# Attention inside a macaron block: the longest row's probabilities turned in squares of 32 by VectorE and moved on chip by 16 DMAs, a group's values weighed at once, the end batches' projections moved

## The chip, the cores and the metric

The kernel runs on one core of one Trainium2 chip. The metric is device time in microseconds (us); the kernel before has a median of 2754.09 us over 3 runs (2752.3 to 2754.87).

## The reference

The input x is 8 batches x 512 tokens x 512 features, all float32. Three stages follow each other:

```
x = x + 0.5 * ffn(layernorm(x))        # gate and up 512 -> 2048, silu, keep 2 of 4, down 2048 -> 512
x = x + attention(layernorm(x))
x = x + 0.5 * ffn(layernorm(x))        # the same weights again

attention: q = x @ w_q.T   (16 heads of 32)        k, v = split(x @ w_kv.T)   (one head, shared)
           q, k scaled and rotated;  a = q k^T, masked causally;  p = softmax(a)
           out = (p @ v) @ w_proj.T + b_proj
```

Only the attention in the middle is touched by this change.

## The kernel before

The engines run programs of their own, in a fixed order, and meet at semaphores. `ffn_phase` makes the first and the third stage; `attention_phase` makes the second.

**Groups, rows and units.** Attention goes through 8 batches. A batch has four groups of 4 heads, and a group has four rows: 128 queries each, of all 4 heads. By causality row i has i + 1 blocks of 128 keys. One (group, row) is a unit K; there are 16 in a batch and 128 in all. `ORDER = (0, 1, 2, 3)`: the shortest row comes first, the longest (row 3, 4 blocks, 512 keys) last.

**A unit's way.** `scores(K)` (PE, L1093): 4 matmuls, one for each head, into banks 0 to 3. `mask_scores` (DVE, L1353): adds the mask and takes the minimum, out to `probs`, one instruction for each head. `exps` (ACT, L1234): the exponential in place, with the sum. `turn_probs(K, j)` (PE, L1102): 4 transposes of 128x128 for block j, into one of three turning banks. `copy_turned`: that bank to `pt`, by ACT (L1239) or by DVE (L1359; `ON_VECTOR` says which blocks). `weigh(K)` (PE, L1117): the values times the turned blocks, 4 matmuls a block, two records each in the trace, into bank 6. After a group's last `weigh`, `scale_output` (DVE, L1372) divides by the sums, which `invert_sums` (DVE, L1365), `widen` (POOL) and `turn_sums` (PE, L1078) have made ready.

**The order of the work.** Every engine has a `step(K)`, written out by hand. PE's is: blocks 0 and 1 of unit K turned; the projection that `PROJECT` gives for this unit of the batch (keys and values of the next batch at unit 0, its queries at 1, 2, 5, 6, the output of the batch before at 9, 10, 13, 14); blocks 2 and up turned; the sums turned in the last unit of a group; at even units `weigh(K - 2)` and `weigh(K - 1)`; and `scores(K + 3)`. DVE's is: two heads of `mask_scores(K + 2)`, its copies, the other two heads, what a projection left in its bank (two instructions for queries, L1342 and L1345; one for an output, L1377), the sums' reciprocal, the scaling, and statistics for a later batch. `scores(K)` waits until all four heads of unit K - 1 are masked, since the banks are the same. `probs` has three buffers, `pt` holds rows 2 and 3 apart from rows 0 and 1.

**Queues.** All DMAs are issued by SP, in program order. In attention these are, for each batch, four stores of the finished x (L902), each after DVE's addition, and one load of a later x (1 MB, L894).

Of the kernel before, what the change touches and what calls it, by code (L numbers as in the profile page):

```python
# [26 lines left out]
P = 128  # L27
# [4 lines left out]
def macaron_kernel(nc, x_in, w_gu, w_d, w_q, w_kv, w_p, b_p, rotary_q, rotary_k, out):  # L32
# [35 lines left out]
    halves = place("halves", [P, TT], F32)  # L68
    stats = place("stats", [P, NB, TT, 6], F32)
# [3 lines left out]
    nmax = place("nmax", [P, 3, TT], F32)  # L73
# [56 lines left out]
    pt = place("pt", [P, 2 * TT, HG, P], F32)  # L130
# [21 lines left out]
    probs = place("probs", [P, 3, HG, S], F32)  # L152
# [7 lines left out]
    with ExitStack() as ctx:  # L160
# [60 lines left out]
        p_turned = sem("p_turned")  # L221
        pt_scalar = sem("pt_scalar")
# [567 lines left out]
        def attention_phase(src, dst, m0):  # L790
# [15 lines left out]
            ORDER = (0, 1, 2, 3)  # L806
            PLACES = ((7,), (5, 6), (0, 1, 2), (3, 4, 5, 6))
            ON_VECTOR = ((), (1,), (1,), (1, 3))
            TURN_X, TURN_KV, TURN_K = {11: 0, 12: 1, 13: 2, 14: 3}, 1, 4
            PROJECT = {0: ("kv", 0), 1: ("q", 0), 2: ("q", 1), 5: ("q", 2), 6: ("q", 3),  # L810
                       9: ("out", 0), 10: ("out", 1), 13: ("out", 2), 14: ("out", 3)}
# [3 lines left out]
            FINISH = {2: 0, 3: 1, 6: 2, 7: 3}  # L815
# [13 lines left out]
            def heads_of(ap):  # L829
                return ap.rearrange("p (h d) -> p h d", d=HD)  # L830

            def blocks_before(K, of):

                one = [sum(1 for j in range(i + 1) if of(i, j)) for i in ORDER]
                return K // TT * sum(one) + sum(one[:K % TT])
# [30 lines left out]
            for K in range(ALL):  # L866
                B, k = divmod(K, UNITS)
                nxt = B + 1
                next_turn("p", K, 0)
                if row_of(K) >= 1:  # L870
                    next_turn("p", K, 1)
                if k in PROJECT:
                    what, t = PROJECT[k]
                    if what == "out":
                        if B > 0:
                            next_turn("out", B - 1, t)
                    elif nxt < BATCHES:
                        next_turn(*(("kv", nxt) if what == "kv" else ("q", nxt, t)))
                for j in range(2, row_of(K) + 1):
                    next_turn("p", K, j)  # L880
# [10 lines left out]
            def sync(sp):  # L891
# [30 lines left out]
                sp.wait_ge(q_finished, BATCHES * NHG)  # L922
                load_raw(0)
                sp.wait_ge(k_step, BATCHES * KSTEP)
                sp.wait_ge(x_biased, BATCHES * TT)
                load_raw(1)
                store(BATCHES - 2)
# [8 lines left out]
            def gpsimd(g):  # L936
# [40 lines left out]
                def step(K):  # L977
# [6 lines left out]
                    if nxt < BATCHES:  # L984
                        if k in FINISH:
                            finish_q(nxt, FINISH[k])
# [33 lines left out]
            def tensor(pe):  # L1020
# [76 lines left out]
                def turn_probs(K, j):  # L1097
# [3 lines left out]
                    for s in range(HG):  # L1101
                        last = pe.transpose(ps[:, s * P:(s + 1) * P], probs[:, K % 3, s, j * P:(j + 1) * P], ident[:, :])  # L1102
                    last.then_inc(p_turned, 1)

                def weigh(K):

                    B, k = divmod(K, UNITS)
                    i = row_of(K)
                    pe.wait_ge(pt_scalar, blocks_before(K + 1, by_scalar))
                    pe.wait_ge(pt_vector, blocks_before(K + 1, by_vector))  # L1110
                    if k % TT == 0 and K >= TT:
                        pe.wait_ge(att_done, K // TT)
                    if k == 0:
                        pe.wait_ge(kvtok_done, B + 1)
                    for j in range(i + 1):
                        for s in range(HG):
                            last = pe.matmul(outs[s * HD:(s + 1) * HD, i * P:(i + 1) * P], kvtok[:, B % 2, j, 1],  # L1117
                                             pt[:, PLACES[i][j], s], start=(j == 0), stop=(j == i))
                    if k % TT == TT - 1:
                        last.then_inc(pv_done, 1)  # L1120
# [13 lines left out]
                def project(B, k):  # L1134

                    if k not in PROJECT:
                        return
                    what, t = PROJECT[k]
                    if what == "out":
                        if B > 0:  # L1140
                            project_out(B - 1, t, take_turn(("out", B - 1, t), x_summed, (B - 1) * TT + t + 1))
                    elif B + 1 < BATCHES:
                        if what == "kv":
                            project_kv(B + 1)
                        else:
                            project_q(B + 1, t)

                def step(K):
                    B, k = divmod(K, UNITS)
                    i, nxt = row_of(K), B + 1  # L1150
                    turn_probs(K, 0)
                    if i >= 1:
                        turn_probs(K, 1)
                    project(B, k)
                    for j in range(2, i + 1):
# [41 lines left out]
                weigh(ALL - 2)  # L1197
# [361 lines left out]
```

## Time and profile before

| | us |
|---|---|
| median of 3 runs | 2754.09 |
| the profiled execution | 2751.58 |
| its span | 2749.7 |
| PE busy | 2710.5 |
| DVE busy | 1852.4 |
| ACT busy | 1122.3 |
| POOL busy | 306.0 |
| granted TensorE clock, mean share | 0.997 |

The profiled execution lies 2.5 us under the median, and its span 1.9 us under its own time. In the span the first stage runs to about 1,090 us, attention to about 1,680 us, and the third stage to the end. A matmul's busy time is longer than the time until the next one starts, since they are pipelined, so a PE that is 99% busy can still have room; what a matmul costs is read from start to start.

The rows below come from the page, from the instructions in order of time (start, length, engine, line, operation, out<-in, and in brackets the idle time before it and what ended it), from tables by stretch (start:end, length, then for PE, PE's weight loads, DVE, ACT and POOL the busy time and the instructions, the granted clock as a share, the DMA engines' share, GB/s), and from the chain that ended last.

### The profile page before, as it was taken

The numbers are of one execution on the slowest core, as the hardware profiler recorded it, in microseconds if no ns is written. First come the engines' busy times: TensorE is split into PE (matmuls) and PEld (weight loads), VectorE is DVE, ScalarE is ACT, GpSimd is POOL, SyncE is SP. The second block draws the span as 40 slices with busy tenths as digits, with TensorE's granted clock in tenths as the row PEclk, the third lists the DMA queues.
The fourth block names the chain that finished last, engine by engine and source line by source line (L and its number), as shares of the span: only waits on it lengthen the run. The fifth ranks groups of instructions, "written<-read, shape, count | busy, mean of one in ns | idle before, by whom it ended". The sixth has DMA issues, their size and how long they took to land.

```text
span 2749.7 us, 41657 instructions
## 1 busy us (share of the span) xinstructions
PE 2710.5 (99%) x15520; PEld 2191.6 (80%) x15520; DVE 1852.4 (67%) x3538; ACT 1122.3 (41%) x2399; POOL 306.0 (11%) x318
## 2 busy tenths in 40 slices
PE   8999999999999999999999999999999999999999
PEld 6888888888888887677777768888888888888887
DVE  6667666765676667777777775667666766676655
ACT  4233333333333233777777784333333332333232
POOL 0000000000000004544444430000000000000000
PEclk9999999999999999999999999999999999999999
DMA  4210311121112111000000012211221132103100
GB/s 147 83 46 16 138 46 46 62 93 46 46 62 92 46 46 60 18 13 28 32 32 28 29 47 93 81 49 46 81 77 58 38 103 82 46 16 107 46 15 31
DMA packets 65069, 156.49 MB, mean 57 GB/s; under 512 B 6784, under 2 KB 7040, under 8 KB 64640
## 3 DMA queue, kind: packets, MB, share of 16 engines
q1 hardware_dynamic: 64896, 154.17, 16.7%
q8 instruction: 111, 1.82, 0.3%
q14 instruction: 62, 0.51, 0.1%
HBM read 128.97 MB, written 25.17 MB: 56 GB/s over the span
## 4 chain that ended last, share of the span: by engine, by line
PE 94%; DVE 3%; ACT 1%; POOL 1%; issue 0%; DMA 0%; SPq 0%; ACTq 0%; DVEq 0%; POOLq 0%
PE bank L391 50%; PE bank L412 25%; PE bank L1102 5%; PE bank L1070 3%; PE bank L1093 3%; PE bank L1117 3%; PE bank L1130 3%; PE bank L274 1%; DVE probs L1353 1%; PE bank L1045 1%; PE bank L1078 1%; POOL xnt_l L974 0%; PE bank L428 0%; DVE att L1372 0%; ACT hs_h L521 0%
## 5 line engine op out<-in xcount | busy, mean ns | idle before, releaser
L391 PE MATMUL bank<-xnt_h,wgu_h 128*128 128x512 f32 x2048 | 802.1, 392 | 4.2 <-ACT sg L507 2.8
L391 PE MATMUL bank<-xnt_h,wgu_l 128*128 128x512 f32 x2048 | 798.0, 390 | 0.0
L391 PE MATMUL bank<-xnt_l,wgu_h 128*128 128x512 f32 x2048 | 797.7, 389 | 0.0
L576 DVE TENSOR_TENSOR h<-bank,sg 128x512 f32<-128x512 f32 x256 | 176.8, 691 | 590.1 <-PE bank L391 574.4
L511 ACT ACTIVATE mag<-h 128x512 f32<-128x512 f32 x256 | 162.0, 633 | 715.6 <-DVE h L576 715.6
L391 PEld LDWEIGHTS bank<-xnt_h,wgu_h 128*128 128x128 f32 x2048 | 385.0, 188 | 84.4 <-ACT sg L507 3.7
L391 PEld LDWEIGHTS bank<-xnt_h,wgu_l 128*128 128x128 f32 x2048 | 384.9, 188 | 80.7
L391 PEld LDWEIGHTS bank<-xnt_l,wgu_h 128*128 128x128 f32 x2048 | 385.1, 188 | 78.3
L412 PE MATMUL bank<-wd_h,hs_h 128*128 128x512 f32 x1008 | 392.2, 389 | 0.0
L412 PE MATMUL bank<-wd_h,hs_l 128*128 128x512 f32 x1008 | 392.1, 389 | 0.0
L412 PE MATMUL bank<-wd_l,hs_h 128*128 128x512 f32 x1008 | 392.1, 389 | 0.0
L521 ACT CAST hs_h<-h 128x512 fp32r<-128x512 f32 x256 | 155.6, 622 | 510.8 <-DVE h L605 503.3
L1234 ACT ACTIVATE probs<-probs,nmax 128x384 f32<-128x384 f32 (+3 forms) x512 | 284.8, 560 | 2.0 <-DVE nmax L1353 1.8
L1353 DVE CUSTOM_DVE_ANT_0 probs<-bank,causal 128x384 f32<-128x384 f32 (+3 forms) x512 | 226.4, 485 | 43.3 <-PE bank L1093 43.0
L507 ACT ACTIVATE sg<-bank 128x512 f32<-128x512 f32 x256 | 153.0, 598 | 207.1 <-PE bank L391 206.6
L412 PEld LDWEIGHTS bank<-wd_h,hs_l 128*128 128x128 f32 x1008 | 189.2, 188 | 39.4
L412 PEld LDWEIGHTS bank<-wd_h,hs_h 128*128 128x128 f32 x1008 | 189.2, 188 | 39.3
L412 PEld LDWEIGHTS bank<-wd_l,hs_h 128*128 128x128 f32 x1008 | 189.2, 188 | 39.0
L281 POOL TENSOR_SCALAR var_eps<-meanvar 128x4 f32<-128x4 f32 x23 | 7.9, 342 | 1786.6 <-DVE meanvar L250 1786.6
L1102 PEld LDWEIGHTS bank<-ident,probs 128*128 128x128 f32 x1280 | 140.2, 142 | 73.7 <-ACT probs L1234 45.3
L1102 PE MATMUL bank<-ident,probs 128*128 128x128 f32 x1280 | 179.8, 282 | 7.0 <-ACT xt_raw L1226 5.2
L563 DVE SCALAR_TENSOR_TENSOR x_sb<-bank,x_sb 128x512 f32<-128x512 f32 (+1 forms) x256 | 159.1, 682 | 11.1 <-PE bank L412 5.8
(132 smaller groups left out, 3221.3 us busy)
## 6 DMA issues: line engine op xcount, KB each, us to landing
raw_gu<-in_w_gu SPq DMA_DIRECT2D x128, 512.0 KB, 4.9
raw_d<-in_w_d SPq DMA_DIRECT2D x128, 256.0 KB, 2.6
x_mid<-x_sb SPq DMA_DIRECT2D x64, 256.0 KB, 2.0
x_sb<-x_mid SPq DMA_DIRECT2D x10, 1024.0 KB, 5.5
x_sb<-in_x SPq DMA_DIRECT2D x32, 256.0 KB, 4.7
out<-x_sb SPq DMA_DIRECT2D x32, 256.0 KB, 2.1
x_sb<-x_mid SPq DMA_DIRECT2D x24, 256.0 KB, 4.9
raw_q<-in_w_q SPq DMA_DIRECT2D x1, 1024.0 KB, 5.0
```

Source lines behind the costliest of these rows:

```text
L391: last = pe.matmul(ps, w[:, r, kind, k], xs[:, b, k], start=(i == 0), stop=(i == 3 * KD - 1))
L412: last = pe.matmul(bank[DOWN + t][:, :], hs[:, b, r, tok], w[:, r], start=(i == 0), stop=(i == 3 * NR - 1))
L507: a.activation(sg[:, r % 2], bank[GATE + r % 2][:, :], ACT.Silu).then_inc(silu_done, 1)
L511: a.activation(mag[:, r], h[:, r], ACT.Abs).then_inc(mag_done, 1)
L521: a.copy(hs_h[:, b, r], h[:, r]).then_inc(hs_h_done, 1)
L563: v.scalar_tensor_tensor(out=x, in0=bank[banks + t][:, :], scalar=0.5, in1=x, op0=ALU.mult, op1=ALU.add).then_inc(added, 1)
L576: v.tensor_tensor(h[:, r], bank[UP + r % 2][:, :], sg[:, r % 2], ALU.mult).then_inc(h_done, 1)
L1070: last = pe.matmul(ps[:, :], w[:, k, cols], x[:, 0, k], start=(k == n == 0), stop=(k == KD - 1 and n == 2))
L1093: last = pe.matmul(bank[SCORES + s][:, 0:width(i)], qt[rows, B % 2, hg, i * P:(i + 1) * P], kt[rows, B % 2, 0:width(i)], start=True, stop= ...
L1102: last = pe.transpose(ps[:, s * P:(s + 1) * P], probs[:, K % 3, s, j * P:(j + 1) * P], ident[:, :])
L1234: a.activation(row, row, ACT.Exp, bias=nmax[:, K % 3, s:s + 1], scale=-1.0, accum_out=sums[:, G % 2, s, i:i + 1]).then_inc(exp_done, 1)
L1353: v.tensor_tensor_reduce(out=probs[:, K % 3, s, 0:w], in0=bank[SCORES + s][:, 0:w], in1=causal[:, S - w:S], scale=1.0, scalar=MASKED, op0= ...
```

## The change

- The rows' order in a group is now (3, 0, 1, 2): the longest first. Each row has a buffer of its own (`probs3`, `probs0`, `probs1`, `probs2`) in place of the three that took turns.
- Row 3 isn't turned by PE any more. Its probabilities are laid out in pieces of 32 keys with the 4 heads side by side. DVE transposes squares of 32x32 in place (`turn_squares`, two instructions of 128x1024 a group). SP then issues 16 DMAs a group (`turn_long`), each 32 partitions x 4 x 128 numbers (64 KB, runs of 512 bytes), from `probs3` to `pt3`, and so puts each square where its transpose belongs. They wait until both DVE instructions are done (`squared`) and until the group before has been weighed (`pv_done`), since `pt3` is single.
- DVE masks the next group's row 3 only when all 16 have landed (`squares_moved`), since `probs3` is single too.
- `weigh(G)` takes a whole group at once, 40 matmuls, in the next group's first unit.
- DVE copies one turned block in a group instead of four, ACT five instead of six.
- In the first batch the queries of the next are projected at units 1, 5, 9, 10 (before: 1, 2, 5, 6), in the last batch the outputs at 2, 5, 9, 13 (before: 9, 10, 13, 14).
- ACT runs one exponential of a single column ahead of attention, and casts two blocks of x before the first exponentials instead of one.

```diff
+            ORDER = (3, 0, 1, 2)
+            LONG = 3
+            PLACES = ((0,), (1, 2), (3, 4, 5))
+            ON_VECTOR = ((), (), (1,))
...
+            FIRST_PROJECT = {0: ("kv", 0), 1: ("q", 0), 5: ("q", 1), 9: ("q", 2), 10: ("q", 3)}
+            LAST_PROJECT = {2: ("out", 0), 5: ("out", 1), 9: ("out", 2), 13: ("out", 3)}
...
+                def turn_long(G):
+                    sp.wait_ge(squared, (G + 1) * 2)
+                    if G > 0:
+                        sp.wait_ge(pv_done, G)
+                    for a in range(TT):
+                        for q in range(TT):
+                            sp.dma_start(pt3[q * 32:(q + 1) * 32, :, a, :, :].rearrange("p j s n -> p j (s n)"),
+                                         probs3[a * 32:(a + 1) * 32, :, :, :].rearrange("p (j q) s n -> p q j (s n)", q=TT)[:, q]
+                                         ).then_inc(squares_moved, 16)
...
-                for B in range(BATCHES - 2):
-                    store(B)
-                    sp.wait_ge(ax_stored, (B + 1) * TT * 16)
-                    load(B + SLOTS)
...
+                for B in range(BATCHES):
+                    for hg in range(NHG):
+                        turn_long(B * NHG + hg)
...
+                    if B > 0:
+                        store(B - 1)
+                    if 0 < B < BATCHES - 1:
+                        sp.wait_ge(ax_stored, B * TT * 16)
+                        load(B + SLOTS - 1)
...
+                def weigh(G):
...
+                    pe.wait_ge(squares_moved, (G + 1) * TT * TT * 16)
+                    for i in ORDER:
+                        if i == ORDER[1]:
+                            pe.wait_ge(pt_scalar, blocks_before(K, by_scalar))
+                            pe.wait_ge(pt_vector, blocks_before(K, by_vector))
+                        for j in range(i + 1):
+                            for s in range(HG):
+                                turned = pt3[:, j, :, s, :] if i == LONG else pt[:, PLACES[i][j], s]
...
-                    if k % 2 == 0 and K > 0:
-                        weigh(K - 2)
-                        weigh(K - 1)
+                    if k % TT == 0 and K > 0:
+                        weigh(K // TT - 1)
...
+                a.activation(warm[:, :], halves[:, 0:1], ACT.Exp)
...
+                    if i == LONG and K >= TT:
+                        v.wait_ge(squares_moved, K // TT * TT * TT * 16)
...
+                def turn_squares(K, half):
+                    v.wait_ge(exp_done, (K + 1) * HG)
+                    n = S // 64
+                    pieces = probs3[:, half * n:(half + 1) * n, :, :].rearrange("p c s n -> p (c s n)")
+                    v.transpose(pieces, pieces).then_inc(squared, 1)
```

PE, the end of the first group of the first batch, before. `probs` turned is L1102, `kt,qt` are the scores, `pt,kvtok` the weighing, `rwide` the sums, `kwide` the next batch's keys:

```order
2841 L1102 MATMUL bank<-ident,probs 128x128 x4
2842 L1117 MATMUL bank<-pt,kvtok 32x128 x12
2843 L1093 MATMUL bank<-kt,qt 128x256 x4
2844 L1102 MATMUL bank<-ident,probs 128x128 x16
2845 L1078 MATMUL bank<-ident,rwide 128x128 x4
2846 L1093 MATMUL bank<-kt,qt 128x384 x4
2847 L1102 MATMUL bank<-ident,probs 128x128 x4
2848 L1061 MATMUL bank<-ident,kwide 128x128 x4
2849 L1117 MATMUL bank<-pt,kvtok 32x128 x28
2850 L1093 MATMUL bank<-kt,qt 128x512 x4
2851 L1102 MATMUL bank<-ident,probs 128x128 x8
```

The same place in the changed kernel; `probs_109`, `probs_91`, `probs_108` are rows 0, 1 and 2, `pt_107` is `pt3`:

```order
2826 L1131 MATMUL bank<-kt,qt 128x512 x4
2827 L1140 MATMUL bank<-ident,probs_91 128x128 x8
2828 L1131 MATMUL bank<-kt,qt 128x128 x4
2829 L1140 MATMUL bank<-ident,probs_108 128x128 x12
2830 L1116 MATMUL bank<-ident,rwide 128x128 x4
2831 L1131 MATMUL bank<-kt,qt 128x256 x4
2832 L1099 MATMUL bank<-ident,kwide 128x128 x4
2833 L1159 MATMUL bank<-pt_107,kvtok 32x128 x16
2834 L1159 MATMUL bank<-pt,kvtok 32x128 x24
2835 L1131 MATMUL bank<-kt,qt 128x384 x4
2836 L1140 MATMUL bank<-ident,probs_109 128x128 x4
```

The 16 transposes of row 3 are gone, and the 12 and 28 weighing matmuls became one run of 40. The scores of the next group's row 3 (128x512) stand ahead of two turned blocks, and the scores of its row 0 (128x128), which need row 3 masked, come right behind these.

DVE in the changed kernel, from the squares of a group to the masking of the next group's row 3, in the second group of the first batch (`probs_106` is `probs3`; an ISA row with `nmax` alone reads the minimum):

```order
785 L1408 STREAM_TRANSPOSE probs_106<-probs_106 128x1024 [waits exp_done]
786 L1399 ISA probs_91,nmax<-bank,causal 128x256 [waits score_done]
790 L1408 STREAM_TRANSPOSE probs_106<-probs_106 128x1024 [waits exp_done]
795 L1425 TENSOR_TENSOR att<-bank,rt 128x512 [waits rt_done,pv_done]
796 L1399 ISA probs_108,nmax<-bank,causal 128x384 [waits score_done]
804 L1382 TENSOR_TENSOR qt<-bank,rot_q 128x512 [waits q_done]
805 L1385 STREAM_SHUFFLE qtmp<-bank 128x512 [waits q_finished]
807 L1399 ISA probs_106,nmax<-bank,causal 128x16x32 [waits squares_moved,score_done]
815 L1418 RECIPROCAL rsum<-sums 128x16 [waits rwide_done,exp_done]
816 L1399 ISA probs_109,nmax<-bank,causal 128x128 [waits score_done]
820 L1412 COPY pt<-bank 128x512 [waits p_turned]
```

Between the squares and the waiting instruction stand one masking of row 2, the scaling of the group before, and what a projection left. Behind it on DVE stand the reciprocal of the sums, the masking of row 0 and the one copy that DVE still makes.

SP in the changed kernel, the first groups of attention and the end of the second batch:

```order
159 L946 DMA pt_107<-probs_106 32x4x128 [waits squared]
160 L946 DMA pt_107<-probs_106 32x4x128 x15
161 L946 DMA pt_107<-probs_106 32x4x128 [waits pv_done,squared]
174 L946 DMA pt_107<-probs_106 32x4x128 x15
175 L925 DMA x_mid<-x_sb 128x512 [waits x_summed] x4
176 L917 DMA x_sb<-x_mid 128x4x512 [waits ax_stored]
177 L946 DMA pt_107<-probs_106 32x4x128 [waits pv_done,squared]
```

Before, SP had only the stores and the load of a batch here; now a group's first DMA waits for the weighing of the group before, and 15 follow it on the same queue.

## Rows read from the trace of the kernel before

**Rows 1.** The page: the chain that ended last, by line.

```profile
PE bank L391 50%; PE bank L412 25%; PE bank L1102 5%; PE bank L1070 3%; PE bank L1093 3%; PE bank L1117 3%; PE bank L1130 3%; PE bank L274 1%; DVE probs L1353 1%; PE bank L1045 1%; PE bank L1078 1%; POOL xnt_l L974 0%; PE bank L428 0%; DVE att L1372 0%; ACT hs_h L521 0%
```

**Rows 2.** Engines by stretch; edges are starts of DVE's scaling L1372, one a group.

```profile
1140.89:1155.90 15.01, 12.05 (x168) 8.92 (x172) 12.05 (x46) 13.49 (x42) 9.17 (x11) 1.00 0.01 2
1155.90:1174.84 18.94, 16.64 (x180) 11.26 (x184) 11.77 (x41) 14.51 (x46) 8.26 (x9) 0.91 0.01 1
1174.84:1544.28 369.44, 362.55 (x3784) 268.18 (x3788) 272.56 (x926) 269.16 (x817) 171.18 (x170) 1.00 0.09 30
1544.28:1615.35 71.07, 69.74 (x748) 52.08 (x752) 54.49 (x186) 52.66 (x162) 34.22 (x34) 1.00 0.12 40
1615.35:1628.88 13.53, 11.21 (x160) 8.04 (x164) 10.86 (x40) 12.61 (x41) 2.49 (x3) 1.00 0.09 32
1628.88:1662.14 33.26, 30.75 (x340) 22.50 (x344) 26.87 (x89) 26.95 (x81) 6.40 (x8) 0.90 0.05 18
1662.14:1676.28 14.14, 14.14 (x153) 11.12 (x154) 7.44 (x16) 8.13 (x20) 2.51 (x3) 1.00 0.32 107
```

**Rows 3.** PE in order of time, the end of a middle batch's first group.

```profile
1332.82 0.86 PE L1117 MATMUL bank<-pt,kvtok 128*32 128x128 f32 x24
1333.61 0.71 PE L1093 MATMUL bank<-kt,qt 32*128 32x256 f32 x8
1334.26 1.99 PE L1102 MATMUL bank<-ident,probs 128*128 128x128 f32 x16
1336.23 0.63 PE L1078 MATMUL bank<-ident,rwide 128*128 128x128 f32 x4
...
1338.69 1.74 PE L1117 MATMUL bank<-pt,kvtok 128*32 128x128 f32 x56
1340.36 1.14 PE L1093 MATMUL bank<-kt,qt 32*128 32x512 f32 x8
```

**Rows 4.** DMA issues by line: operation, count, KB each, median us to landing.

```profile
x_mid<-x_sb SPq DMA_DIRECT2D x64, 256.0 KB, 2.0
raw_kv<-in_w_kv SPq DMA_DIRECT2D x1, 128.0 KB, 2.0
```

**Rows 5.** SP's queue in order of time, where it issues without waits.

```profile
1732.58 3.96 SPq L317 DMA_DIRECT2D x_sb<-x_mid  x8
...
1095.52 0.94 SPq L894 DMA_DIRECT2D x_sb<-x_mid  x2
```

**Rows 6.** DVE in order of time, the same group as in rows 3.

```profile
1324.49 0.69 DVE L1353 CUSTOM_DVE_ANT_0 probs<-bank,causal 128x512 f32<-128x512 f32 x1
1325.10 0.69 DVE L1359 COPY pt<-bank 128x512 f32<-128x512 f32 x1
...
1330.55 0.28 DVE L1353 CUSTOM_DVE_ANT_0 probs<-bank,causal 128x128 f32<-128x128 f32 x1
1330.77 0.29 DVE L1307 TENSOR_TENSOR krot<-kvtok,rot_k 128x128 f32<-128x128 f32 x1
...
1331.75 0.43 DVE L1333 COPY kwide<-krot 128x512 f32<-128x512 f32 x1
1332.49 0.69 DVE L1342 TENSOR_TENSOR qt<-bank,rot_q 128x512 f32<-128x512 f32 x1 [0.31 <-PE bank L1070]
...
1333.11 0.74 DVE L1345 STREAM_SHUFFLE qtmp<-bank 128x512 f32<-128x512 f32 x1
1333.74 0.23 DVE L1365 RECIPROCAL rsum<-sums 128x16 f32<-128x16 f32 x1
```

**Rows 7.** The chain that ended last, in order of time: one projection of queries.

```profile
1329.70 2.75 PE bank L1070 x12
```

**Rows 8.** PE in order of time, where it waits for masked scores in the first batch.

```profile
1145.88 0.50 PE L1093 MATMUL bank<-kt,qt 32*128 32x128 f32 x8 [2.96 <-DVE nmax L1353]
...
1160.25 0.50 PE L1093 MATMUL bank<-kt,qt 32*128 32x128 f32 x8 [1.89 <-DVE nmax L1353]
```

**Rows 9.** Engines by stretch, right behind the second wait of rows 8.

```profile
1161.77:1165.18 3.41, 3.23 (x37) 2.04 (x34) 1.36 (x6) 2.81 (x10) 1.42 (x3) 0.50 0.00 0
```

More of the change, by code:

```diff
@@ L68, in macaron_kernel @@
     halves = place("halves", [P, TT], F32)
+    warm = place("warm", [P, 1], F32)
     stats = place("stats", [P, NB, TT, 6], F32)
@@ L827, in att_of, with blocks_of, row_of_head, in_pieces @@
                 return (xnt_h[:, 1], xnt_l[:, 1]) if B % 2 == 1 else (att2_h[:, :, :], att2_l[:, :, :])
-            def heads_of(ap):
-                return ap.rearrange("p (h d) -> p h d", d=HD)
+            def blocks_of(i):
+                return 0 if i == LONG else i + 1
+            def row_of_head(K, s):
+                i = row_of(K)
+                return probs3[:, :, s, :] if i == LONG else probs_of[i][:, s, :]
+            def in_pieces(ap):
+                return ap.rearrange("p (c n) -> p c n", n=32)
             def blocks_before(K, of):
-                one = [sum(1 for j in range(i + 1) if of(i, j)) for i in ORDER]
+                one = [sum(1 for j in range(blocks_of(i)) if of(i, j)) for i in ORDER]
                 return K // TT * sum(one) + sum(one[:K % TT])
@@ L868, in attention_phase @@
                 nxt = B + 1
[L869 to L879, printed above, removed]
+                for j in range(min(blocks_of(row_of(K)), 2)):
+                    next_turn("p", K, j)
+                if k in project_in(B):
+                    what, t = project_in(B)[k]
+                    next_turn(*(("out", B - 1, t) if what == "out" else ("kv", nxt) if what == "kv" else ("q", nxt, t)))
+                for j in range(2, blocks_of(row_of(K))):
                     next_turn("p", K, j)
@@ L1101, in turn_probs @@
                     for s in range(HG):
-                        last = pe.transpose(ps[:, s * P:(s + 1) * P], probs[:, K % 3, s, j * P:(j + 1) * P], ident[:, :])
+                        last = pe.transpose(ps[:, s * P:(s + 1) * P], probs_of[row_of(K)][:, s, j * P:(j + 1) * P], ident[:, :])
                     last.then_inc(p_turned, 1)
[L1105 to L1113, printed above, removed]
-                        pe.wait_ge(kvtok_done, B + 1)
[L1115 to L1120, printed above, removed]
+                def weigh(G):
+                    K = G * TT + TT
+                    B, hg = divmod(G, NHG)
+                    if G > 0:
+                        pe.wait_ge(att_done, G)
+                    if hg == 0:
+                        pe.wait_ge(kvtok_done, B + 1)
+                    pe.wait_ge(squares_moved, (G + 1) * TT * TT * 16)
[6 more added lines that the diff above has]
+                                turned = pt3[:, j, :, s, :] if i == LONG else pt[:, PLACES[i][j], s]
+                                last = pe.matmul(outs[s * HD:(s + 1) * HD, i * P:(i + 1) * P], kvtok[:, B % 2, j, 1],
+                                                 turned, start=(j == 0), stop=(j == i))
+                    last.then_inc(pv_done, 1)
                 def project_out(B, t, ps):
@@ L1134, in project @@
                 def project(B, k):
-                    if k not in PROJECT:
+                    if k not in project_in(B):
                         return
-                    what, t = PROJECT[k]
+                    what, t = project_in(B)[k]
                     if what == "out":
[L1140 to L1146, printed above, removed]
+                        project_out(B - 1, t, take_turn(("out", B - 1, t), x_summed, (B - 1) * TT + t + 1))
+                    elif what == "kv":
+                        project_kv(B + 1)
+                    else:
+                        project_q(B + 1, t)
                 def step(K):
                     B, k = divmod(K, UNITS)
[L1150 to L1153, printed above, removed]
+                    blocks, nxt = blocks_of(row_of(K)), B + 1
+                    for j in range(min(blocks, 2)):
+                        turn_probs(K, j)
                     project(B, k)
-                    for j in range(2, i + 1):
+                    for j in range(2, blocks):
                         turn_probs(K, j)
@@ L1258, in step @@
                     nxt = B + 1
-                    mine = [j for j in range(row_of(K) + 1) if by_scalar(row_of(K), j)]
+                    mine = [j for j in range(blocks_of(row_of(K))) if by_scalar(row_of(K), j)]
                     if nxt < BATCHES:
@@ L1379, in drain_projection @@
                 def drain_projection(B, k):
-                    if k not in PROJECT:
+                    if k not in project_in(B):
                         return
-                    what, t = PROJECT[k]
-                    if what == "q" and B + 1 < BATCHES:
+                    what, t = project_in(B)[k]
+                    if what == "q":
                         split_q(B + 1, t)
-                    if what == "out" and B > 0:
+                    if what == "out":
                         add_output(B - 1, t, bank_of["out", B - 1, t])
```

76 lines of the change are left out of this document (47 added, 29 removed).

## The prediction, on record before the changed kernel ran

> **What bounds the kernel now.** I read the chain that ended last first. Half of it is L391 and a quarter L412, the two feed-forward stages [rows 1], which the change doesn't touch. What it touches is L1102, 5% of the chain, with L1117 and L1093 around it. So the whole case is decided in the attention stage, some 590 us.
>
> Next I read the engines by stretch, cut where DVE scales a group's output [rows 2]. Five whole batches take 369.44 us, 73.9 each, and PE is busy in 362.55 of them: in the middle batches PE is the bound, with DVE and ACT both at about 0.73. The sixth, which ends without a projection of keys and values, takes 71.07. At the ends it is different: one group of the first batch takes 15.01 us with PE busy for 12.05, one of the last takes 13.53 with 11.21. Those groups are bound by the waits between engines, and they are short because little or nothing is projected in them.
>
> **What goes.** The 16 transposes of row 3 run from 1334.26 to 1336.23, 1.97 us [rows 3]. 32 groups of them are 63 us of PE's time, and that would be the gain if nothing new were waited for. The weighing costs what it did: 24 records in 0.79 us and 56 in 1.67 [rows 3], 2.46 us a group, now in one piece. DVE loses three copies of 0.69 us and gains two transposes of 128x1024, which the trace doesn't show. From below they can't take less than twice the 0.43 of the copy that goes from SBUF to SBUF with 512 columns, 0.86; from above I take twice the 0.74 of the STREAM_SHUFFLE with 512 columns, 1.5 [rows 6]. I take 1.15, so DVE's load stays about what it was. ACT loses one copy.
> The Trainium skill (Vector Engine (DVE) Microarchitecture Reference, section 3.8) says that the transpose mode sustains one element per cycle per lane; at the 0.96 GHz that Trainium Kernel Development and Optimization gives for VectorE (section NeuronCore Architecture) that is an estimate of 1.07 us for 1024 columns. No row here shows it.
>
> **What comes: one new loop.** The edits that matter are three waits. SP's 16 DMAs wait for the weighing of the group before. DVE's masking of the next row 3 waits for all 16. And PE's scores of the next row 0 wait for that masking, since the banks are shared. Behind PE's wait stand row 2's transposes, the sums, the scores of row 1 and the next weighing, which releases the next 16 DMAs. So it closes on itself, once a group. I walk it from 0, where PE has finished weighing.
> - The DMAs: the first starts at about 0.15. SP's issues without waits come 8 in 3.96 us, 0.495 each, and the two with three dimensions take 0.94 together, 0.47 each [rows 5]. I take 0.49, so the sixteenth starts at 0.15 + 15 x 0.49 = 7.5. A DMA of 128 KB or of 256 KB lands 2.0 us after its issue [rows 4]; these are 64 KB with both ends on chip, so I take 1.8. All have landed at T = 9.3. Bounds: 0.43 (a bare issue, below any of these rows' means) and a landing of 1.2 give 7.8; 0.55 (a third dimension costing more than the two rows show) and 2.0 give 10.4.
> - DVE masks four heads of 512, one every 0.61 [rows 6]: PE sees it at T + 2.5.
> - Meanwhile PE has had two projections of 2.75 [rows 7], the scores of rows 2 and 3 (by their width 0.9 and 1.1, since row 1's take 0.65) and twelve transposes (1.97 / 16 each) [rows 3]: 9.0 us. It therefore stands from 9.0 to T + 2.5 = 11.8, nearly 3 us. This is a wait that isn't there today.
> - On DVE, behind the masking: 1.25 for the queries' two instructions (1332.49 to 1333.74), 0.24 for the reciprocal, four maskings of 128 at 0.22, one copy, at the maskings' pace 0.61 [rows 6]; end at T + 5.5. The scores of row 1 take 0.65 [rows 3], the weighing 2.46: the loop closes at T + 8.7.
> - A group that drains an output there instead of queries is 0.6 shorter, one that drains nothing 1.2.
> The squares don't lengthen it: DVE can start on them at T + 5.5 or, behind a statistic, 6.1, needs 2 x 1.15 and 0.7 for two maskings between, and ends by T + 8.5 to 9.1, where the weighing is just done. At 1.5 each they would add 0.6 us a group.
> The Trainium skill names both sides of the price. DMA: Bandwidth & Descriptors, Issuing engines are not separate DMA queues, calls the issuing time "usually small relative to the DMA itself"; here, by rows 5, it is 7.4 of the 9.2 us. Its Rules for kernel authors say that a transfer under 64 KB is mostly overhead and should be merged into a larger one, which speaks against sixteen of them.
>
> **The sum.** A middle batch is 4 (T + 8.7), less 2 x 0.6 for the two groups with outputs, plus what lies on the loop once a batch: the keys' rotation on DVE (1330.77 to 1332.18, 1.4) [rows 6], the projection of keys and values (12 matmuls, 2.75, as rows 7), two blocks turned (0.5 each) and one normalising of a block of x, also 0.5. That is 4T + 39.0 = 76.2 against 73.9: +2.3, five times, 11.5. The sixth batch lacks one projection: 73.5 against 71.07, +2.4. The first batch's groups: T + 7.5 = 16.8, as before; then T + 9.2 = 18.5 against 15.01, because two projections of queries now stand where none did, and the 9.3 us of moves have to pass anyway; then T + 10.7 = 20.0 against 18.94: +4.6. The last batch: T + 8.1 = 17.4 against 13.53; two groups with 34.1 against 33.26; the last, where nothing is masked any more, T + 2.6 = 11.9 against 14.14: +2.5 [rows 2]. Together +21 us. The start I cost at nothing: a first masking of 512 in place of 128 (+1.6) stands against no turning before the keys' projection and an exponential made ready early; either side of 0 by 2 us. The load and stores of x land in the gap that SP has at a batch's end (the last store can be issued at T + 3, the load some 2.5 later, and the next moves not before T + 11).
>
> **The clock.** PE waited 2.96 and 1.89 us for masked scores in the first batch [rows 8]; right behind the second wait the granted clock was 0.5 (1.2 GHz) for 3.41 us [rows 9], and rows 2 show 0.91 and 0.90 in the groups with such waits and 1.00 in the others. After the change some 28 groups have a wait of nearly 3 us. If one in three is followed by such a drop, and what PE has left in the loop (transposes, scores, weighing, some 4.5 us) loses 0.9 us in it, that is 9 or 10 x 0.9 = 8 us. Bounds: none, and all 28 (25).
> So the profiled execution comes to 2751.6 + 21 + 8 = 2781; the median of the runs shown is 2.5 above, 2783.
>
> **The rivals.**
> *The moves land in time.* For: the figures in the sum balance at T = 8.6 without the clock, only 0.7 under what I take, and an issue of a small on-chip DMA isn't in the trace. Against: it needs 0.44 an issue where rows 5 show 0.47 and 0.495. The place is the same wait, DVE's masking of row 3: below T = 8.3 the kernel is faster by over 0.2%. At 7.8, without clock drops, it is 21 - 1.5 x 30 = -24: 2730. In the extreme, with T under 6.5, PE stays the bound and the 63 us come: 2691; that needs 0.3 an issue.
> *It comes out even.* T between 8.3 and 8.6, or the clock's loss given back at the start and the end: 2754, where the two sides of the sum cancel.
> *The moves or squares are slower than a row shows.* DMAs of 512-byte runs between 32 partitions could take longer in the engines than SP needs to issue them, or DVE could need two cycles an element, 2.2 us a transpose. Two of those are 2 us more in each group, past where the weighing ends: +1.5 x 30 = 45 on top of 29; and T = 11.5 makes 66 on top. 2830 to 2850. Against: the DMA engines are 9% busy in rows 2, and nothing there is slow by number of packets.
>
> **How the numbers follow.** I give the forecast 0.46, the moves in time 0.30, even 0.13, much slower 0.11. What differs by less than 0.2% (5.5 us) a measurement of this kernel can't tell from no change. The range goes from 2732 (the first rival at its bound T) to 2826 (T = 10.4, +33, and half the groups with a clock drop); the likeliest case alone holds 2765 to 2805. Faster by over 0.2%: 0.31; within: 0.13; slower: 0.56.
>
> **What would show it.** SP's queue: groups of 16 issues, one start every 0.49, the last landing 9.3 us after the weighing. The waits: DVE's masking of row 3 ended by a DMA, some 3 us in each group, and PE's scores behind it waiting on DVE. The table by stretch: 76 us a middle batch with PE busy for less of it, 17 to 18 us for groups of the first and the last batch. The granted clock at 0.5 after some of the waits. It would be wrong if the issues came at 0.44 or less, if the landing were near 1.2, or if DVE came to the masking later than the DMAs do.

## The result and the profile after

| | before | after |
|---|---|---|
| median (us) | 2753.82 (4 runs) | 2951.1 (4 runs, 2948.38 to 2952.43) |
| ratio, with its 95% interval | | 1.072 (1.0707 to 1.0733) |
| span of the profiled execution | 2749.7 | 2949.4 |
| granted clock, mean | 0.997 | 0.954 |

The kernel is 7.2% slower: the direction that I gave 0.56, and far outside the range. All of it is lost in attention. The page shows where: SP's queue, which no line of [rows 1] names, is a tenth of the chain that ended last, and the clock is low in the slices of attention and there alone.

```profile
PEclk9999999999999998788888888999999999999999
PE 80%; SPq 10%; DVE 4%; DMA 2%; issue 2%; ACT 1%; POOL 1%; DVEq 0%; ACTq 0%
PE bank L398 47%; PE bank L419 23%; SPq L946 10%; PE bank L1159 2%; DMA pt<-probs 2%; PE bank L1140 2%; DVE probs L1399 2%; PE bank L1131 2%; PE bank L281 1%; PE bank L1083 1%; PE bank L1116 1%; PE bank L1171 0%; POOL xnt_l L1012 0%; PE bank L435 0%; DVE probs L1408 0%
```

The table by stretch, cut at the same groups' scalings as [rows 2]. The third row is the five whole batches, 98.4 each where they were 73.9; PE is busy in 374 us of 492 and the granted clock is 0.84, which between 1 and 0.5 means a third of the time at 1.2 GHz.

```profile
1151.16:1174.21 23.05, 17.26 (x172) 13.16 (x172) 15.47 (x53) 12.54 (x39) 10.12 (x11) 0.85 0.18 47
1174.21:1203.47 29.26, 17.79 (x164) 11.38 (x168) 11.95 (x41) 14.57 (x44) 9.07 (x10) 0.71 0.15 37
1203.47:1695.25 491.78, 373.99 (x3464) 272.03 (x3468) 278.03 (x906) 261.54 (x795) 171.06 (x170) 0.84 0.23 65
1695.25:1792.08 96.83, 72.43 (x684) 53.79 (x688) 55.66 (x182) 52.00 (x158) 34.19 (x34) 0.82 0.23 66
1792.08:1814.51 22.43, 13.73 (x152) 10.22 (x152) 11.77 (x40) 12.50 (x37) 2.49 (x3) 0.85 0.33 95
1814.51:1860.12 45.61, 27.67 (x304) 20.47 (x304) 27.88 (x88) 25.65 (x79) 6.45 (x8) 0.81 0.18 47
1860.12:1874.90 14.78, 10.75 (x129) 8.70 (x129) 4.33 (x15) 6.63 (x18) 2.52 (x3) 0.92 0.56 168
```

The new loop is there as it was drawn. Here is one turn of it: SP, then DVE, then PE, each in order of time.

```profile
1302.23 10.61 SPq L946 DMA_DIRECT2D pt<-probs  x16
```

```profile
1314.38 0.69 DVE L1399 CUSTOM_DVE_ANT_0 probs<-bank,causal 128x512 f32<-128x512 f32 x1 [6.67 <-DMA pt<-probs]
...
1321.53 1.23 DVE L1408 STREAM_TRANSPOSE probs<-probs 128x1024 f32<-128x1024 f32 x1
```

```profile
1302.05 0.93 PE L1131 MATMUL bank<-kt,qt 32*128 32x384 f32 x8
...
1316.97 0.81 PE L1131 MATMUL bank<-kt,qt 32*128 32x128 f32 x8 [5.40 <-DVE nmax L1399]
1317.71 2.95 PE L1140 MATMUL bank<-ident,probs 128*128 128x128 f32 x12
...
1323.33 2.39 PE L1159 MATMUL bank<-pt,kvtok 128*32 128x128 f32 x80
```

The weighing ends at 1302.05, the first move is issued 0.18 later, the sixteenth ends its issue at 1312.84, and DVE masks at 1314.38: T = 12.3, not 9.3. PE waits 5.4 us, not 3, and then makes 12 transposes in 2.95 us, twice what they take at full clock (16 took 1.97 in [rows 3]). All 512 issues of the line (min, median, max in ns), and the time from an issue's start to its landing:

```profile
L946 SPq DMA_DIRECT2D pt<-probs x512: 585/601/1966, 1105.9 to 1869.2; - x171
...
DMA to landing us min/median/max: 2.0/2.0/3.6
```

The stretch behind the wait, its columns as above:

```profile
1316.10:1322.92 6.82, 5.95 (x34) 4.39 (x35) 6.68 (x25) 4.76 (x16) 3.15 (x4) 0.50 0.00 0
1322.92:1330.00 7.08, 7.08 (x112) 5.39 (x114) 5.16 (x19) 5.27 (x19) 4.41 (x4) 1.00 0.19 48
```

The waits in sum (us in all, times, longest), PE's and DVE's:

```profile
PE bank L1131 <- DVE nmax L1399: 191.7, 47, 9.1
```

```profile
DVE probs L1399 <- DMA pt<-probs: 204.7, 31, 9.0
```

To compare runs I cut each group in three: T, from the end of a weighing to the next masking of row 3; R, from there to the start of the next weighing; and the weighing, 2.39. T and R are means over the 30 groups that have both, read from the instructions in order of time; the last column is R over the 20 groups of the five whole batches alone, since the forecast's R is for a middle batch: (39.0 - 4 x 2.46) / 4 = 7.3. All kernels but the changed one have one run here, and runs of one kernel lie up to 6 us apart.

| kernel | T | R | us | R, middle batches |
|---|---|---|---|---|
| forecast | 9.3 | | 2783 | 7.3 |
| after | 12.4 | 9.6 | 2951 | 9.9 |
| half the bytes in each move | 12.1 | 9.6 | 2945 | 10.0 |
| PE kept busy in the wait | 12.7 | 8.5 | 2928 | 8.6 |
| x turned in other units | 12.4 | 8.8 | 2927 | 8.9 |
| eight moves | 7.3 | 8.6 | 2766 | 8.9 |
| own buffer, masking made to wait | 12.3 | 10.2 | 2970 | 10.6 |

In the changed kernel T is 0.14 us to the first issue, 10.07 from the first issue to the sixteenth (15 steps of 0.67) and 2.16 from there to the masking.

### The profile page after: what moved, and what is told of

Same layout as the page of the kernel before. It is cut to its first block, busy times and chain, and to the rows that moved or that the text cites. A ratio compares the mean times of both kernels' runs of the same rounds, so it can differ in the third digit from the quotient of the medians.

```text
span 2949.4 us, 41072 instructions
## 1 busy us (share of the span) xinstructions
PE 2724.9 (92%) x15008; PEld 2195.9 (74%) x15008; DVE 1862.6 (63%) x3506; ACT 1111.1 (38%) x2368; POOL 306.0 (10%) x318
## 4 chain that ended last, share of the span: by engine, by line
PE 80%; SPq 10%; DVE 4%; DMA 2%; issue 2%; ACT 1%; POOL 1%; DVEq 0%; ACTq 0%
PE bank L398 47%; PE bank L419 23%; SPq L946 10%; PE bank L1159 2%; DMA pt<-probs 2%; PE bank L1140 2%; DVE probs L1399 2%; PE bank L1131 2%; PE bank L281 1%; PE bank L1083 1%; PE bank L1116 1%; PE bank L1171 0%; POOL xnt_l L1012 0%; PE bank L435 0%; DVE probs L1408 0%
## 5 line engine op out<-in xcount | busy, mean ns | idle before, releaser
L1399 DVE CUSTOM_DVE_ANT_0 probs<-bank,causal 128x256 f32<-128x256 f32 (+3 forms) x512 | 222.9, 482 | 220.4 <-DMA pt<-probs 204.7
L1270 ACT ACTIVATE probs<-probs,nmax 128x256 f32<-128x256 f32 (+3 forms) x512 | 284.2, 559 | 166.2 <-DVE nmax L1399 166.0
L1131 PE MATMUL bank<-kt,qt 32*128 32x512 f32 (+3 forms) x1024 | 124.9, 566 | 192.0 <-DVE nmax L1399 191.7
L1131 PEld LDWEIGHTS bank<-kt,qt 32*128 32x128 f32 x1024 | 50.6, 232 | 228.5 <-DVE nmax L1399 207.0
```

Source lines behind the costliest of these rows:

```text
L1131: last = pe.matmul(bank[SCORES + s][:, 0:width(i)], qt[rows, B % 2, hg, i * P:(i + 1) * P], kt[rows, B % 2, 0:width(i)], start=True, stop= ...
L1270: a.activation(row, row, ACT.Exp, bias=nmax[:, i, s:s + 1], scale=-1.0, accum_out=sums[:, G % 2, s, i:i + 1]).then_inc(exp_done, 1)
L1399: v.tensor_tensor_reduce(out=row_of_head(K, s), in0=scored, in1=mask, scale=1.0, scalar=MASKED, op0=ALU.add, op1=ALU.min, accum_out=nmax[: ...
```

## The experiments

**Half the bytes in each move.** From the second group on, key blocks 2 and 3 are left where they are.

```
+ js = TT if G == 0 else 2
...
- sp.dma_start(pt3[q * 32:(q + 1) * 32, :, a, :, :] ..., probs3[...] ...[:, q] ...)
+ sp.dma_start(pt3[q * 32:(q + 1) * 32, 0:js, a, :, :] ..., probs3[...] ...[:, q, 0:js] ...)
```

> The changed kernel, whose 16 moves a group carry only key blocks 0 and 1 from the second group on: the same number of moves with half the bytes and half the packets (it leaves out the moves of key blocks 2 and 3). Theory (SP's issuing sets the time of the moves: 0.64 us each, 16 of them 10.2): the issues keep their pitch, and the kernel stays at 2940 to 2955. Rival (bytes or 512-byte packets in the DMA engines set it): the issues come closer, T falls from 12.3 to 7 or 8, and the kernel comes to about 2790.

Measured: 2945.4 us, one run. All 512 issues of the line (min, median, max in ns) and their landing:

```profile
L947 SPq DMA_DIRECT2D pt<-probs x512: 585/597/1878, 1106.2 to 1864.1; - x171
...
DMA to landing us min/median/max: 1.8/1.9/3.4
```

In the changed kernel the median was 601. With half the bytes and half of the moves' packets T falls by 0.2 us a group, most of it in the landing, and the kernel by 6 us, no more than runs of one kernel differ: bytes and packets in the DMA engines are not the limit, SP's issuing is.

**Eight moves a group**, from the second group on; the moves of the upper 64 partitions are left out, and the two waits for the moves count eight.

```
- for a in range(TT):
+ for a in range(TT if G == 0 else 2):
...
```

> The changed kernel with 8 moves a group in place of 16 from the second group on (it leaves out the moves of the upper 64 partitions of probabilities). Theory (number of issues times 0.64): 8 issues take 5.1 us less, T falls from 12.3 to about 7.2. By the sum of the prediction a middle batch would be 4 x 7.2 + 39 = 68, and the waits of TensorE and the clock's drops go with it: 2710 to 2740. Rival (what bounds the loop is something else than the moves, such as the masking, the squares or the order on VectorE): above 2850.

Measured: 2766.0 us, one run. Eight issues less take 5.1 us off T and 185 us off the kernel. The rival (something else bounds the loop, above 2850) is ruled out. But my 2710 to 2740 was missed by 26: a batch takes 74.5 (mean of five) and not 68, because R in these batches is 8.9 where the forecast has 7.3. So a second error was left in R, to be found apart from the moves.

**PE kept busy in the wait**: 44 transposes of the identity into a bank that nobody reads.

```
+ if FILL and k % TT == 2 and K + AHEAD < ALL:
+     ...
+     for n in range(FILL):
+         pe.transpose(turning[b][...], ident[:, :], ident[:, :])
  if K + AHEAD < ALL:
      scores(K + AHEAD)
```

> The changed kernel with 44 transposes of the identity added on TensorE in each group, ahead of the scores that wait for row 3's masking (into a bank that nobody reads then). They occupy the engine during the wait, and nothing else changes. Theory (of the time lost, some 77 us come from the clock, which the granted clock of the changed kernel shows at 0.5 for about 259 us of the attention stage, always behind that wait): the clock stays at 1.0 through nearly all of the attention stage, a middle batch falls from 98 to about 89 us, the kernel to about 2875 (2860 to 2890). First rival (what follows the wait isn't limited by TensorE, so the clock costs nothing): 2951 or some more, the clock at 1.0. Second rival (the drop doesn't hang on the wait): the clock shows 0.5 as before and the time stays.

Measured: 2927.9 us, one run, granted clock 0.988. The same place in PE's order, with 4.97 us of filler:

```profile
1304.19 4.97 PE L1211 MATMUL bank<-ident 128*128 128x128 f32 x44
1310.00 0.51 PE L1132 MATMUL bank<-kt,qt 32*128 32x128 f32 x8 [0.84 <-DVE nmax L1405]
```

The clock stays up when the wait is filled (0.97 in the five whole batches, where it was 0.84), so the drop does hang on the wait; but that gives 23 us and not 77, and a middle batch 94.9 and not 89. R falls by 1.08 a group; T was 0.31 longer in this run, half of it in the issues and the rest in the landing, for a reason that I haven't found. So the clock's own price is an estimate: about 1.08 x 30 = 32 us. Some 250 us at half clock (a third of the stage) cost that little. One part of the reason is in the trace of this run: PE at full clock comes earlier and then waits for DVE, 1.05 us for `qtmp` at 1312.58, two transposed blocks behind the row above. The other is argued, not shown: PE's projections at half clock lie in the stretch where it would wait for the moves anyway.

**x turned in other units**: 10, 11, 12, 14 in place of 11 to 14. It came from two rows of the changed kernel, of ScalarE and GpSimd in order of time, in the group that projects keys and values:

```profile
1290.88 0.58 ACT L1262 COPY xt_raw<-bank 128x512 f32<-128x512 f32 x1 [3.70 <-POOL xnt_l L1012]
```

```profile
1288.28 0.61 POOL L997 COPY rwide<-rsum 128x512 f32<-128x512 f32 x1 [10.29 <-DVE rsum L1418]
1288.83 0.61 POOL L1010 CAST xnt_h<-xt_raw 128x512 fp32r<-128x512 f32 x1
1289.53 1.26 POOL L1012 TENSOR_TENSOR xnt_l<-xt_raw,xnt_h 128x512 fp32r<-128x512 f32 x1
```

GpSimd's cast of a block that was long there stands behind the widening of the sums, which waits 10.3 us for DVE's reciprocal, which stands behind the masking that waits for the moves. ScalarE's copy of the next block waits for GpSimd, and behind it stand two exponentials of row 3, which the squares need.

> The changed kernel with the turning of the next x block by block in units 10, 11, 12 and 14 in place of 11 to 14, and nothing else. In its trace ScalarE waits 3.7 us once a batch, ahead of row 3's exponentials, for GpSimd's part of the block turned in unit 13; GpSimd stands behind the widening of sums, which waits for VectorE, which waits for the moves. Theory (that wait is why the group with the projection of keys and values needs 14 to 15 us from the first masking to the weighing, where the prediction's sum has about 10): the wait goes, that group gets 2 to 3.7 us shorter, the kernel 2951 - 7 x 3 = 2930 (2922 to 2938). Rival (the masking and the squares on VectorE end last there anyway): 2948 to 2955.

Measured: 2926.9 us, one run: as the theory said. R falls by 0.7 a group; the group in question goes from 29.1 to 25.5 (29.2 to 25.5 in the mean of five).

**The end batches' projections alone**, in the kernel before.

```
+ FIRST_PROJECT = {0: ("kv", 0), 1: ("q", 0), 5: ("q", 1), 9: ("q", 2), 10: ("q", 3)}
+ LAST_PROJECT = {2: ("out", 0), 5: ("out", 1), 9: ("out", 2), 13: ("out", 3)}
...
```

> The kernel before with one part of the change alone: in the first batch the projections of queries stand in other units (0, 1, 5, 9, 10), and in the last batch those of outputs (2, 5, 9, 13). Theory (this part is worth little, since it only spreads the same work over groups that were bound by waits between engines): 2 to 6 us faster than before. Rival (the spread lengthens the groups that it goes to by what it takes from others): within 1 us of before.

Measured: 2748.87 (11 runs), ratio 0.9982 (0.9973 to 0.9991): 5 us, as expected. In the kernel before, this part of the change is a small gain; the loss lies elsewhere.

**A buffer of its own for the squares**, so that masking needn't wait for the moves.

```
- qt = place("qt", [P, 2, NHG, S], F32)
+ squares3 = place("squares3", [P, TT, TT, HG, 32], F32)
+ qt = place("qt", [P, QSLOTS, S], F32)
...
-     v.wait_ge(squares_moved, K // TT * TT * TT * 16)        # in mask_scores
+     v.wait_ge(squared, K // TT * 2)
...
- v.transpose(pieces, pieces).then_inc(squared, 1)            # in turn_squares
+ if K >= TT:
+     v.wait_ge(squares_moved, K // TT * TT * TT * 16)
+ v.transpose(squares3[...] ..., probs3[...] ...).then_inc(squared, 1)
```

More than the buffer changes here: to make room, queries are kept in five slots (`QSLOTS`) and `qtmp` in one, and with that queries and outputs are projected in other units.

> The changed kernel with a buffer of its own for the squares: VectorE turns row 3 out of place, the 16 moves (the same form, runs of 512 bytes) read from there, and the next row 3 is masked without waiting for them. Room comes from keeping queries in five slots in place of eight and one qtmp in place of two, so queries are projected in units 1, 3, 5, 10 (first batch 1, 5, 7, 10) and outputs in 6, 9, 13, 14. Theory (the loss hangs on the wait that the shared bank and the shared buffer make, not on the moves themselves): 16 issues take 10 to 12 us of a group of 16 and are hidden, TensorE bounds again, a middle batch is 73.9 - 8 = 66 to 68 us, the clock stays up, and the kernel comes to 2700 (2690 to 2725). First rival (waits between VectorE, ScalarE and TensorE bound the group at 73 or more without the transposes too): 2745 to 2765. Second rival (the moves themselves bound: a round of weighing, moves, weighing): above 2850.

Measured: 2767.3 us, one run. 184 us come back with all 16 moves still made, although the room for the buffer has a price of its own (19 us, by the run that waits again, below). So the loss hangs on the wait. But TensorE doesn't bound again; a batch takes 75 us, not 66 to 68, and PE waits 51.3 us in all for masks. Of the two rivals the first came true, 2 us over its range.

**The same with long runs**: each move one run of 2 KB a partition on both sides.

```
- sp.dma_start(pt3[q * 32:(q + 1) * 32, :, a, :, :] ..., squares3[a * 32:(a + 1) * 32, :, q, :, :] ...)
+ sp.dma_start(pt3[q * 32:(q + 1) * 32, a, :, :, :] ..., squares3[a * 32:(a + 1) * 32, q, :, :, :] ...)
...
```

> As own_buffer, and the squares are written in an order in which each move takes one run of 2 KB a partition on either side (two dimensions in place of three; VectorE's transpose writes with three dimensions). Theory: an issue takes about 0.47 us in place of 0.64 (what the issues with fewer dimensions took in the kernel before), but since the moves are hidden the time is own_buffer's within 5 us, some 2700. Rival (the transpose gets slower with the broken-up output): own_buffer's plus 10 to 30 us.

Measured: 2763.5 (5 runs), ratio 1.0038 (1.0023 to 1.0052). The time is within 5 us of the run before, as forecast (the 2700 that stood beside it was not); the issue doesn't get cheaper, 0.59 and not 0.47.

```profile
L947 SPq DMA_DIRECT2D pt<-squares x512: 507/591/1951, 1105.2 to 1682.7; - x171
...
DMA packets 89644, 190.03 MB, mean 69 GB/s; under 512 B 14976, under 2 KB 15232, under 8 KB 89216
```

**The same, with the masking made to wait for the moves again.**

```
      v.wait_ge(squared, K // TT * 2)
+     v.wait_ge(squares_moved, K // TT * TT * TT * 16)
```

> As own_long, but VectorE's masking of the next row 3 waits for the moves as in the changed kernel. So it is the changed kernel with cheaper issues and other units for projections. Theory (the issue's price by its dimensions is the mis-sized term): the pitch falls to about 0.47, T to 9.3 from 12.3, and the kernel to about 2951 - 30 x 3 = 2860, less a part of the clock's loss: 2810 to 2860. Rival (every on-chip move costs 0.64 to issue, whatever its dimensions): T stays at 12, 2930 to 2960.

Measured: 2970.2 us, one run. T is 12.3: the rival is right, these moves cost 0.63 from start to start by the median with two dimensions, 0.64 with three. The time lies 10 us over the rival's range, and against the changed kernel it prices the room that the own buffer took, the queries' units and slots together: R 10.2 against 9.6, 19 us.

**Whole lanes**: 4 moves of 256 KB, each partition to itself (values not moved across partitions).

```
+ if G > 0:
+     for a in range(TT):
+         sp.dma_start(pt3[:, a, :, :, :] ..., probs3[:, a * TT:(a + 1) * TT, :, :] ...)
+     return
...
```

> The changed kernel, whose moves from the second group on are 4 of 256 KB over all 128 partitions, each partition to itself (it leaves out the change of partition, so the values are not those of the reference). It asks what makes an issue cost 0.60 us here against 0.34 to 0.46 for loads and stores between the chip's memory and SBUF: first theory (both ends on chip, whatever the shape): 0.60 again, T = 0.15 + 3 x 0.64 + 2.3 = 4.4. Second (the 32 partitions): 0.34 to 0.46, T = 3.9. Either way the masking doesn't wait for moves; the extreme of the prediction's first rival says 2691 for T under 6.5. With what the other runs showed of the loop without moves (own buffer: 2767) I expect 2745 to 2765.

Measured: 2748.0 us, one run.

```profile
L946 SPq DMA_DIRECT2D pt<-probs x124: 464/603/2222, 1128.2 to 1662.9; - x124
...
DMA to landing us min/median/max: 2.2/2.4/4.6
```

The first theory holds: 0.60 with 128 partitions as with 32, 256 KB as 64, two dimensions as three. What these issues have in common is that both ends are on chip. That it is this, and nothing else that they share, is not shown, and they are not the only dear ones: the bias, a load from the chip's memory that is spread over all partitions, took 0.66 in the kernel before.

```profile
L912 SPq DMA_DIRECT2D bias<-in_b_p x1: 662/662/662, 994.4 to 994.4; - x1
```

And with four moves in place of sixteen, a batch is still 72.3 (mean of five), with T at 6.4, which the moves no longer set: T under 6.5 does not give 2691.

**Own buffer and x turned apart**: the kernel with long runs, x turned in units 10, 11, 12 and 14.

> own_long with the turning of the next x in units 10, 11, 12 and 14 (two parts tried one by one so far). Theory (the wait of ScalarE for GpSimd once a batch is worth as much here as it was in the changed kernel, 24 us there): 2763 - 24 = 2740 (2732 to 2750), the group with keys and values down from 24.4 us to about 21. Rival (in a group that doesn't wait for moves something else ends as late): 2755 to 2765.

Measured: 2734.5 (4 runs), ratio 0.9938 (0.9923 to 0.9953). A batch falls from 75.0 to 69.7, the group with keys and values from 24.4 to 19.1, further than the 21 that I wrote. The granted clock goes from 0.96 to 1.00 in these batches with it; how much of the gain is the clock's is not shown.

**And the squares after the maskings of row 1.**

```
- turn_squares(K, 0); mask_scores(K + 2, (0, 1)); turn_squares(K, 1); mask_scores(K + 2, (2, 3))
+ mask_scores(K + 2, (0, 1)); mask_scores(K + 2, (2, 3)); turn_squares(K, 0); turn_squares(K, 1)
```

(The calls of row 3's unit, four lines of the kernel drawn into one.)

> As own_turns, and in row 3's unit VectorE does both transposes after all four maskings of row 1 in place of between them. TensorE waits there 1.2 us a group for the last masking. Theory (the two transposes stand in that wait's way): up to 1.2 x 32 = 38 us less than own_turns; since the moves now start about 1 us later and the shortest group has little over, I expect 20 to 30: 2715 (2700 to 2735), under both kernels. Rival (later squares delay the moves and TensorE waits for these instead): equal to own_turns or slower.

Measured: 2729.3 (5 runs), ratio 0.9918 (0.9904 to 0.9931). 5 us of the 20 to 30. PE's waits in this kernel:

```profile
PE bank L1132 <- DVE nmax L1400: 33.8, 26, 4.3
...
PE bank L1160 <- DMA pt<-squares: 8.4, 7, 4.6
PE bank L1141 <- ACT probs L1271: 7.6, 8, 1.3
```

The wait for masks shrank from 50.5 us to 33.8, but waits for moves (3.0 before this edit) and for exponentials (4.2) grew: the rival holds in part. Still it beats both kernels, the one before by 0.8%.

**The kernel before with the same two small moves** (end batches, x turned apart).

> The kernel before with the end batches' projections moved (measured alone: 5 us faster) and the turning of x in units 10, 11, 12 and 14. In the kernel before, ScalarE's waits for GpSimd's part of x are 12.8 us in 8. Theory (this stall is large only where VectorE, and with it GpSimd, waits for moves): 2749 as without the turning, within 3. Rival (the stall is on the path there too): 2735 to 2742.

Measured: 2746.07 (11 runs), ratio 0.9978 (0.9969 to 0.9987). Within the 3 us of the theory, just. By the medians the turning of x is worth 3 us there; by the ratios (0.9982 without it, 0.9978 with it, each against its own runs of the kernel before) it can't be told from nothing. With the own buffer it was 29. ScalarE's waits for GpSimd are 12.8 us in the kernel before and 34.4 in the one with the own buffer, so "only where VectorE waits for moves" was too narrow: with the own buffer no masking waits for moves, and the stall is there. Of the 63 us of transposes, the squares bring 2746 - 2729 = 17 at best here.

## Why the prediction was wrong, point by point

- **What goes**: the 16 transposes went, and DVE's square transposes took 1.23 to 1.25 us, where I took 1.15 and the estimate beside it said 1.07. Right but for that.
- **The new loop**: right in place, order and cause. The three waits, what stands behind them, and the closing by the next weighing are in the trace. PE has had its work by 9.5 us after the weighing (I wrote 9.0). That SP's stores and load land in the gap at a batch's end was right: no group's first move starts later than 0.51 us after the weighing. The direction, slower, had 0.56 and came true for the reason given, the moves, but the measured loss is nearly seven times the forecast one. "The moves land in time" was wrong; the moves slower than a row shows (0.11) was the nearest rival, with T = 11.5, but for another reason (the engines; it was SP) and still too small (2830 to 2850).
- **The step that failed first: "I take 0.49, so the sixteenth starts at 7.5."** An issue between two on-chip buffers takes 0.60, and 0.64 from start to start by the median, 0.67 in the mean of a group. [rows 5] are loads from the chip's memory; I carried them over to a kind of issue that no row showed, and put my upper bound (0.55) 0.06 above what I took for a third dimension, which costs 0.01 in the runs. The trace of before held an issue of 0.66, the bias. Of the 3.07 us by which T is longer, 2.7 are the issues and 0.36 the end, 2.16 from the sixteenth issue to the masking where I took 1.8. With T = 12.4 in my own sum, 31 groups x 3.07 = 95 us more.
- **The clock**: I took one in three waits followed by a drop, at 0.9 each. Every one is: all 30 waits of PE over 4 us in the changed kernel's attention are followed by a granted clock of 0.50 to 0.61 in the next 4 us. Its price is some 32 us by the filled wait, where I had 8 and a bound of 25. The longer wait (5.4 us in place of 3) isn't what made the drop the rule: of the waits of 2 to 4 us, 8 of 9 were followed by it with eight moves and 9 of 11 with the own buffer. One in three was too low for the wait that I forecast as well.
- **A term that was missing**: ScalarE's 3.7 us for GpSimd, once a batch, 24 us by the run with x turned in other units. I walked PE's and DVE's queues behind their waits, but not GpSimd's, whose first instruction waits for DVE.
- **The account.** The sum without its clock term was 2773. Of the 178 us from there to 2951, T is 95, the clock 32, GpSimd's queue 24, the start of attention 4.5 (the first scaling at 1128.6 for 1124.0). This takes the parts as if they added up, which no run with two of them shows. Some 23 us I haven't traced to one cause. About 7 of them lie in the middle batches (R is 9.85 there; the forecast's 7.3, 1.24 for the clock and 0.98 for GpSimd leave 0.3 a group), the rest in the others. Two slips in the sum itself are small: its terms for a middle batch add up to 4T + 39.25, not 39.0, and the upper end of the range to 2821, not 2826.
- **The extreme rival (2691 with T under 6.5)** was wrong too. With four moves, eight, or an own buffer the kernel comes to 2748 to 2767, and with all that was tried on top to 2729: waits of PE for DVE's maskings (51.3 us with the own buffer, 33.8 in the last kernel) and for the other engines take up much of what the transposes leave. That was only seen by removing the first bound.

## What to carry to other kernels

Price an issue by a row of its own kind: here the moves with both ends on chip cost more than the loads of x, and with sixteen of them in a row an error is counted fifteen times. Without such a row, the dearest kind of issue in the trace is a better upper bound than the nearest one. When a new wait is put on an engine, walk every queue that waits for that engine, GpSimd's too, down to what it holds up elsewhere. A DMA that takes longer than its cover belongs behind a buffer of its own: that was worth 184 of the 197 us lost here.

## What the runs showed of the hardware

- SP's issue of a DMA within SBUF took 0.59 to 0.60 us by the median in eleven kernels, for 32 KB, 64 KB and 256 KB, 32 and 128 partitions, runs of 512 bytes and of 2 KB; loads of x took 0.35 to 0.39 and stores 0.34 to 0.46 by the median in the same traces. It landed 1.9 us after its start with 32 KB, 2.0 with 64 KB and 2.4 with 256 KB.
- A third of the stage at half clock (some 250 us) cost about 32 us, an estimate from the run with the filled wait.
- VectorE wrote the squares in three dimensions (own buffer with long runs) as fast as in one, 1.24 us by the median.
